# Second layer's edge-relation rows: one bf16 product over 48 rows in place of an f32 product over 16

## The chip, the cores and the metric

One core of one Trainium2 chip runs the whole program. The metric is the device time of one execution in microseconds; the time of the kernel before is a median of three runs. A profile is one further execution, taken by the hardware profiler.

## What is computed

Four graph layers on 6,250 nodes of 128 features, with 206,250 edges sorted by destination. After each of the first three layers `x = layernorm(x + layer(x))`; the last adds its layer likewise.

- Layer 0 is attention over the edges of each node (GAT), layer 3 a filter made from 50 edge attributes (SchNet).
- Layer 1 (GCN) gathers the row of each edge's source and sums by destination: `out = segment_sum(dinv[src]*dinv[dst]*h[src], dst)`.
- Layer 2 (HGT) is attention with eight heads, in which every edge has one of 16 relation types:

```python
attn = einsum('ehd,ehd->eh', Q[edge_dst], K[edge_src])
attn = attn * rel_scale[edge_rel] / sqrt(DH)      # rel_scale is 16 x 8, DH is 16
```

The change concerns `rel_scale[edge_rel] / sqrt(DH)`, eight numbers for each edge. They depend on no node, and the kernel makes them ahead of layer 2, while layer 1's edges are summed.

## The kernel before

Edges are taken in 1,616 tiles of 128, in 101 rounds of 16 tiles (`ROUND`). A round has four slots (`SLOTS`) of four tiles (`KT`). All five engines run programs of their own, tied by semaphores; each layer's edge stage is a block of such programs between barriers. Every program is in the kernel twice, for narrow and wide windows of destinations (`either`); in the profiled execution it was the narrow one, a straight list of 101 rounds.

The edge stage of layer 1 (lines 1102 to 1270), per round:

- GpSimd issues 16 indirect DMAs (line 1153), one for each tile, each fetching 128 rows of `gcn_table` by `src_idx`. The target is a ring of eight slots, two rounds deep; before it refills a slot it waits on `agg`, which TensorE raises when the sums of that slot are done.
- SyncE loads the round's 2,048 relation types, broadcast to 16 partitions (`load_types`, line 1131), into one of two buffers: partitions 0 to 15 or 32 to 47 of `types`. A buffer is refilled after VectorE has read it (`ty_done`). Ahead of the stage's loop SyncE also loads the weights of layer 2 (lines 1136 to 1139).
- VectorE compares the types with the partition's number (`edge_types`, line 1215), giving a one-hot `oh16` in f32, 16 rows by 2,048, again at partitions 0 or 32; compares destinations for the one-hot `oh` of 128 by 2,048 (`edge_onehot`, line 1210); and adds the round's sums from PSUM to the accumulator `AC` (line 1228).
- TensorE first makes the relation rows: 16 products, one for each tile, of `oh16` (16 rows by 128 edges) with the table `rel_rows` (16 rows by 8), line 1169, then raises `rel_mm`. Then come the round's sums: 16 products of gathered rows with one-hots, 128 by 128, line 1181, each slot after its gathers (`gath`). Both are f32, and an f32 product stands in the trace as two pairs of weight load (PEld) and matmul (PE); 16 products are 32 of each. TensorE waits besides for `ty_done`, `rel_kept` (a PSUM buffer copied out), `oh_done` and `acc_step` (a PSUM bank added).
- ScalarE copies the relation rows out of PSUM (line 1199) and stores them to `relation_rows` every four rounds.

The table comes in at the start of the program (line 265), is scaled by 1/4 there by VectorE (line 391), and is copied once more to partitions 32 to 47 at the head of the edge stage (line 1264). At that head VectorE also clears buffers and makes the rows of node types (`type_rows`, lines 1238 to 1253), all before the first `edge_types`.

Of the kernel before, what the change touches and what calls it, by code (L numbers as in the profile page):

```python
# [16 lines left out]
BF16 = mybir.dt.bfloat16  # L17
I32 = mybir.dt.int32
U32 = mybir.dt.uint32
ALU = mybir.AluOpType  # L20
# [3 lines left out]
P = 128  # L24
# [5 lines left out]
NR = -(-E // (P * ROUND))  # L30
# [8 lines left out]
NC = -(-(N + P) // CN)  # L39
# [15 lines left out]
NTYPE, NREL, NG = 8, 16, 50  # L55
TY = 64 + NTYPE
# [52 lines left out]
def build(nc, a, out):  # L109
    ctx = ExitStack()  # L110
    with ctx:
# [24 lines left out]
        def sems(name, n=SLOTS):  # L136
            return [sem(f"{name}{b}") for b in range(n)]
# [56 lines left out]
        rel_rows = rows[:, 2 * P:2 * P + H2]  # L194
        rel = rel_rows[0:NREL, :]
# [21 lines left out]
        ld_x, ld_rel = sems("start_x", NC), sem("start_rel")  # L217
# [37 lines left out]
        with nc.Block() as block:  # L255
            @block.sync
            def _(sp):
# [7 lines left out]
                sp.dma_start(rel, a["L2_gnn_rel_scale"]).then_inc(ld_rel, 16)  # L265
# [71 lines left out]
            def _(dve):  # L337
# [52 lines left out]
                dve.wait_ge(ld_rel, 16)  # L390
                s.mark(dve.tensor_scalar(rel, rel, 1.0 / float(np.sqrt(C2)), None, ALU.mult))
# [624 lines left out]
        with nc.Block() as block:  # L1016
# [56 lines left out]
            def _(dve):  # L1073
# [16 lines left out]
                with dve.Fori(0, NC) as c:  # L1090
# [3 lines left out]
                    for j in range(PARTS):  # L1094
# [8 lines left out]
        ty_ready, ty_done, rel_mm, rel_kept, rel_stored = (sems("gcn_edge_types", 2), sem("gcn_type_onehot"), sem("gcn_rel_product"), sem("gcn_rel_kept"),  # L1103
                                                           sems("gcn_rel_stored", 2))
        A = Arena(TMP, 0, TW)
# [3 lines left out]
        types = A.take(RW, parts=2 * 32, dtype=I32)  # L1109
        oh16 = A.take(RW, parts=2 * 32)  # L1110
# [10 lines left out]
        iota_ps, rel_iota = PS[3][:, 1, 0:P], PS[3][:, 1, P:P + 1]  # L1121
        rel_ps = [PS[2][:, j, 0:ROUND * H2].rearrange("p (t h) -> p t h", h=H2) for j in range(2)]

        def kind_rows(par):
            return slice(32 * par, 32 * par + NREL)

        with nc.Block() as block:
            @block.sync
            def _(sp):
                def load_types(i):  # L1130
                    sp.dma_start(types[kind_rows(i % 2), :], a["rel_row"][0, i * RW:(i + 1) * RW].partition_broadcast(NREL)).then_inc(ty_ready[i % 2], 16)

                for i in range(2):
                    load_types(i)
# [8 lines left out]
                for i in range(NR - 2):  # L1143
                    sp.wait_ge(ty_done, i + 1)
                    load_types(i + 2)
# [11 lines left out]
            def _(pe):  # L1157
# [5 lines left out]
                def program(narrow):  # L1163
                    def round_(j, i, par, last):
# [3 lines left out]
                        for t in range(ROUND):  # L1168
                            m = nc.tensor.matmul(rel_ps[par][:, t, :], oh16[kind_rows(par), t * P:(t + 1) * P], rel_rows[kind_rows(par), :], start=True, stop=True)  # L1169
# [38 lines left out]
            def _(dve):  # L1208
# [4 lines left out]
                def edge_types(j, i, par):  # L1213
                    dve.wait_ge(ty_ready[par], 16 * (j + 1))
                    dve.tensor_tensor(oh16[kind_rows(par), :], types[kind_rows(par), :], rel_iota[kind_rows(par), :].to_broadcast([NREL, RW]), ALU.is_equal).then_inc(ty_done, 1)

                def program(narrow):
                    def round_(j, i, par, last):
                        if not last:
                            dve.wait_ge(rel_mm, i + 1)  # L1220
                            edge_types(j + par, i + 1, 1 - par)
                            dve.wait_ge(agg, (i + 1) * SLOTS)
                            edge_onehot(i + 1, 1 - par)
# [10 lines left out]
                    edge_types(0, 0, 0)  # L1234
                    edge_onehot(0, 0)
                    rounds(dve, round_, narrow)

# [1074 lines left out]
```

## Time and profile before

| | us |
|---|---|
| median of 3 runs | 11,816.71 (11,815.05 to 11,828.76) |
| profiled execution, time | 11,788.6 |
| profiled execution, span from first to last instruction | 11,786.7 |
| TensorE matmuls busy | 6,487.3 (55%) |
| GpSimd busy | 6,158.0 (52%) |
| TensorE weight loads busy | 5,541.6 (47%) |
| VectorE busy | 4,881.6 (41%) |
| ScalarE busy | 1,784.6 (15%) |

No engine is busy throughout, since four edge stages with different limits follow each other. In order of time the gathers of the four run from 52 to 3,112, 3,486 to 5,810, 5,966 to 8,713 and 9,194 to 11,632 us; the second is the one that is changed. Busy shares of the whole span say little about it, and it has to be read by itself. Matmul ends in the trace are modelled, so the time at which TensorE had really finished is better read from the engine that waited for it.

### The profile page before, as it was taken

Reading aid. Unit: us, or ns where it says so; the run is one execution under the profiler, and the core shown is the slowest. Engines: PE = TensorE matmul, PEld = TensorE weight load, DVE = VectorE, ACT = ScalarE, POOL = GpSimd, SP = SyncE. Lnnn points to the kernel's source line nnn. Section 1 sums busy time; section 2 is a strip of 40 time slices with the busy share of each in tenths; the row PEclk is TensorE's granted clock in tenths of the full one; section 3 lists DMA queues with packets and bytes.
Section 4 is the critical chain, followed back from the end, with each engine's and each line's share of the span. In section 5 each row is a group of like instructions: output and inputs, shape, how many; then the busy total and the mean of one; then the engine's idle time right before and its main releaser. Section 6 shows DMA issues by size and latency. Waiting matters only on the chain. (4 is left out here: it accounts for less than half of the span.)

```text
span 11786.7 us, 95611 instructions
## 1 busy us (share of the span) xinstructions
PE 6487.3 (55%) x31067; PEld 5541.6 (47%) x31067; DVE 4881.6 (41%) x10538; ACT 1784.6 (15%) x2785; POOL 6158.0 (52%) x6479
## 2 busy tenths in 40 slices
PE   4555555555435555555544445444443677777775
PEld 4444444444425555555434444444432455555553
DVE  4444444444552222222345555555555344444444
ACT  0000000000110000000110000000011444444443
POOL 4544544554216666666445555555530566666663
PEclk6666666666555555555566666666655677777776
DMA  4222222222111111111133433333320222222221
GB/s 132 72 75 74 73 75 75 72 75 75 42 26 55 54 55 55 54 55 54 44 123 121 124 121 119 121 120 122 120 69 1 65 62 61 61 60 61 62 61 38
DMA packets 388329, 878.63 MB, mean 75 GB/s; under 512 B 134341, under 2 KB 202872, under 8 KB 368224
## 3 DMA queue, kind: packets, MB, share of 16 engines
q0 software_dynamic: 232704, 536.56, 16.5%
q1 hardware_dynamic: 150242, 324.95, 8.3%
q10 hardware_dynamic: 4896, 11.01, 0.2%
q8 instruction: 258, 4.23, 0.1%
q14 instruction: 229, 1.88, 0.1%
HBM read 839.65 MB, written 32.40 MB: 74 GB/s over the span
## 5 line engine op out<-in xcount | busy, mean ns | idle before, releaser
L621 POOL DMA_INDIRECT PM<-gat_table,src_idx x1616 | 1529.1, 946 | 1579.9 <-PE ps L660 1070.4
L2081 POOL DMA_INDIRECT TMP<-schnet_table,src_idx x1616 | 1563.3, 967 | 1355.5 <-DVEq L2183 481.8
L1595 POOL DMA_INDIRECT PM<-hgt_kv_table,src_idx x1616 | 1531.4, 948 | 1371.3 <-PE ps L1627 752.0
L1153 POOL DMA_INDIRECT PM<-gcn_table,src_idx x1004 | 953.0, 949 | 463.8 <-issue 288.6
L1169 PE MATMUL ps<-rows,xT 16*128 16x8 f32 x3232 | 625.6, 301 | 716.3 <-issue 696.0
L1169 PEld LDWEIGHTS ps<-rows,xT 16*128 16x128 f32 x3232 | 646.2, 277 | 702.8 <-issue 671.7
L1153 POOL DMA_INDIRECT TMP<-gcn_table,src_idx x612 | 578.6, 945 | 702.4 <-POOLq L1016 373.9
L2108 PE MATMUL ps<-PM 128*128 128x128 f32 x3232 | 627.8, 357 | 539.6 <-issue 402.7
L2108 PEld LDWEIGHTS ps<-PM 128*128 128x128 f32 x3232 | 571.7, 266 | 582.3 <-issue 581.9
L1627 PE MATMUL ps<-PM 128*128 128x136 f32 x3232 | 608.8, 353 | 337.5 <-DVE PM L1716 322.1
L1228 DVE TENSOR_TENSOR AC<-AC,ps 128x128 f32 x101 | 29.2, 289 | 1829.8 <-remote 1437.0
L639 PE MATMUL ps<-PM 128*128 128x4 f32 x3232 | 697.6, 339 | 101.9 <-issue 71.9
L1627 PEld LDWEIGHTS ps<-PM 128*128 128x128 f32 x3232 | 557.8, 253 | 374.6 <-DVE PM L1702 345.1
L639 PEld LDWEIGHTS ps<-PM 128*128 128x128 f32 x3232 | 662.3, 304 | 134.1 <-issue 90.1
L1610 PE MATMUL ps<-TMP 128*128 128x128 f32 x3232 | 654.2, 367 | 59.0 <-issue 24.4
L660 PE MATMUL ps<-PM 128*128 128x137 f32 x3232 | 644.2, 377 | 0.3 <-issue 0.3
L1610 PEld LDWEIGHTS ps<-TMP 128*128 128x128 f32 x3232 | 585.5, 271 | 91.0 <-issue 37.8
L2153 DVE TENSOR_TENSOR PM<-ps,TMP 128x512 f32<-128x512 f32 x404 | 277.2, 686 | 830.9 <-remote 609.4
L660 PEld LDWEIGHTS ps<-PM 128*128 128x128 f32 x3232 | 618.7, 281 | 3.0 <-issue 0.3
L2091 PE MATMUL ps<-PM,WA 50*128 50x512 f32 x808 | 595.3, 825 | 11.1 <-DMA PM<-in_attrT 11.1
L689 PE MATMUL ps<-ident,TMP 64*128 64x64 f32 x101 | 36.8, 365 | 1011.3 <-DVE TMP L813 844.4
L2098 PEld LDWEIGHTS ps<-WA,PM 128*128 128x128 f32 x3232 | 566.2, 246 | 35.8 <-issue 14.8
(374 smaller groups left out, 10772.4 us busy)
## 6 DMA issues: line engine op xcount, KB each, us to landing
PM<-local_dst_row SPq DMA_DIRECT2D x101, 1024.0 KB
PM<-local_dst_row SPq DMA_DIRECT2D x202, 512.0 KB
PM<-in_attrT SPq DMA_DIRECT2D x101, 400.0 KB
PM<-gat_table,src_idx POOLq DMA_INDIRECT x1616
PM<-hgt_kv_table,src_idx POOLq DMA_INDIRECT x1616
TMP<-schnet_table,src_idx POOLq DMA_INDIRECT x1616
PM<-gcn_table,src_idx POOLq DMA_INDIRECT x1004
xT<-in_rel_row SPq DMA_DIRECT2D x101, 128.0 KB
```

The lines of the kernel that those rows point to most:

```text
L621: pool.indirect_dma_start(out=g[:, par, t, 0:ROW0], out_offset=None, in_=tab0_d, in_offset=bass.IndirectOffsetOnAxis(ap=src_idx[:, i * ROU ...
L639: m = nc.tensor.matmul(adp[:, t * H0:(t + 1) * H0], ohT[:, b % 2, k * P:(k + 1) * P], window_of(narrow, adw, i, b, k), start=True, stop=True)
L660: m = nc.tensor.matmul(PS[1][:, bank, 0:GW], o, row_, start=start, stop=stop)
L1153: pool.indirect_dma_start(out=g[n % DEEP][:, k, :], out_offset=None, in_=tab1_d, in_offset=bass.IndirectOffsetOnAxis(ap=src_idx[:, n * KT ...
L1169: m = nc.tensor.matmul(rel_ps[par][:, t, :], oh16[kind_rows(par), t * P:(t + 1) * P], rel_rows[kind_rows(par), :], start=True, stop=True)
L1595: pool.indirect_dma_start(out=g[:, par, t, 0:2 * P], out_offset=None, in_=kv_d, in_offset=bass.IndirectOffsetOnAxis(ap=src_idx[:, i * ROUN ...
L1610: m = nc.tensor.matmul(q_ps[b % 2][:, k, :], ohT[:, b % 2, k * P:(k + 1) * P], window_of(narrow, qw, i, b, k), start=True, stop=True)
L1627: m = nc.tensor.matmul(sums_ps, o, row_, start=b % 2 == 0 and k == 0, stop=b % 2 == 1 and k == KT - 1)
L2081: pool.indirect_dma_start(out=g[:, b, k, :], out_offset=None, in_=tab3_d, in_offset=bass.IndirectOffsetOnAxis(ap=src_idx[:, (i * SLOTS + b ...
L2091: nc.tensor.matmul(zb[b], w1, attr[:, par, b * KT * P:(b + 1) * KT * P], start=True, stop=True).then_inc(z_mm, 1)
L2098: m = nc.tensor.matmul(wb[b % 2][:, k, :], soft[:, b % 2, k * P:(k + 1) * P], w2, start=False, stop=(k == KT - 1), skip_group_check=True)
L2108: m = nc.tensor.matmul(sb_[bank][:, c:c + P], msg[:, b % 2, k, :], oh[:, b % 2, k, :], start=start, stop=stop)
```

## The change

1. The table. It is no longer loaded and scaled at the start of the program. At the head of the edge stage SyncE loads it three times, to rows 0 to 15, 16 to 31 and 32 to 47 of `rel`. `rel_pieces` scales it and splits it in place: `relb` is its value in bf16; what that leaves over is taken on in rows 16 to 47, and what is left over once more in rows 32 to 47. The three groups of rows then hold three bf16 pieces whose sum is the f32 value exactly.
2. The product. One bf16 product over 48 rows in place of the f32 product over 16 rows: 16 products a round as before.
3. The one-hot of types is 48 rows by 2,048 in bf16 (each of the three groups the same), in two buffers by free position. VectorE's compare has the same length and reads types as int32 as before.
4. The types are broadcast to 48 partitions in place of 16, into a single buffer in place of two; a load is issued when VectorE has read the one before it.

```diff
-        types = A.take(RW, parts=2 * 32, dtype=I32)
-        oh16 = A.take(RW, parts=2 * 32)
+        types = A.take(RW, parts=KINDS, dtype=I32)
+        oh16 = A.take(2, RW, parts=KINDS, dtype=BF16)
+        rel, relf, relb = A.take(H2, parts=KINDS), A.take(H2, parts=KINDS), A.take(H2, parts=KINDS, dtype=BF16)
...
-                    sp.dma_start(types[kind_rows(i % 2), :], a["rel_row"][0, i * RW:(i + 1) * RW].partition_broadcast(NREL)).then_inc(ty_ready[i % 2], 16)
-
-                for i in range(2):
-                    load_types(i)
+                    sp.dma_start(types, a["rel_row"][0, i * RW:(i + 1) * RW].partition_broadcast(KINDS)).then_inc(ty_ready, 16)
+
+                for j in range(PIECES):
+                    sp.dma_start(rel[j * NREL:(j + 1) * NREL, :], a["L2_gnn_rel_scale"]).then_inc(rel_ld, 16)
+                load_types(0)
...
-                for i in range(NR - 2):
+                for i in range(NR - 1):
                     sp.wait_ge(ty_done, i + 1)
-                    load_types(i + 2)
+                    load_types(i + 1)
...
-                            m = nc.tensor.matmul(rel_ps[par][:, t, :], oh16[kind_rows(par), t * P:(t + 1) * P], rel_rows[kind_rows(par), :], start=True, stop=True)
+                            m = nc.tensor.matmul(rel_ps[par][:, t, :], oh16[:, par, t * P:(t + 1) * P], relb, start=True, stop=True)
...
-                    dve.wait_ge(ty_ready[par], 16 * (j + 1))
-                    dve.tensor_tensor(oh16[kind_rows(par), :], types[kind_rows(par), :], rel_iota[kind_rows(par), :].to_broadcast([NREL, RW]), ALU.is_equal).then_inc(ty_done, 1)
+                    dve.wait_ge(ty_ready, 16 * (i + 1))
+                    dve.tensor_tensor(oh16[:, par, :], types, rel_iota.to_broadcast([KINDS, RW]), ALU.is_equal).then_inc(ty_done, 1)
...
+                def rel_pieces():
+                    s = Steps(dve, rel_done)
+                    for j in range(2):
+                        s.link(dve.tensor_scalar(above[:, j:j + 1], iota_p[0:KINDS, :], float((j + 1) * NREL), -1.0, ALU.is_ge, ALU.mult))
+                    s.link(dve.scalar_tensor_tensor(kind, above[:, 0:1], float(NREL), iota_p[0:KINDS, :], ALU.mult, ALU.add))
+                    s.mark(dve.scalar_tensor_tensor(rel_iota, above[:, 1:2], float(NREL), kind, ALU.mult, ALU.add))
+                    dve.wait_ge(rel_ld, 16 * PIECES)
+                    s.link(dve.tensor_scalar(rel, rel, 1.0 / float(np.sqrt(C2)), None, ALU.mult))
+                    for j in range(PIECES - 1):
+                        s.link(dve.tensor_copy(relb, rel))
+                        s.link(dve.tensor_copy(relf, relb))
+                        s.link(dve.scalar_tensor_tensor(rel, relf, above[:, j:j + 1], rel, ALU.mult, ALU.add))
+                    s.link(dve.tensor_copy(relb, rel))
...
-                for par in range(2):
-                    dve.tensor_copy(rel_iota[kind_rows(par), :], iota_p[0:NREL, :]).then_inc(acc_step, 1)
-                dve.tensor_copy(rel_rows[kind_rows(1), :], rel).then_inc(acc_step, 1)
-                dve.wait_ge(acc_step, 5)
-                dve.sem_inc(acc_step, 3)
+                dve.wait_ge(acc_step, 2)
+                dve.sem_inc(acc_step, 6)
+                rel_pieces()
                 dve.sem_inc(rel_mm, 1)
                 type_rows()
```

## Rows read from the trace of the kernel before

**Rows 1.** Two stretches: us; busy (count) of PE, PEld, DVE, ACT, POOL; PEclk, DMA, GB/s.
```profile
52.00:3112.00 3060.00, 1584.52 (x8173) 1466.27 (x8173) 1268.12 (x3785) 145.22 (x695) 1528.47 (x1616) 0.61 0.25 75
3486.00:5811.00 2325.00, 1320.77 (x6409) 1276.04 (x6409) 500.39 (x322) 26.62 (x100) 1531.69 (x1616) 0.59 0.19 55
```

**Rows 2.** Waits, 3520 to 5830 us: who waited <- for what: total us, times, longest.
```profile
PE ps L1169 <- issue: 696.0, 676, 2.6
...
POOL PM L1153 <- issue: 284.9, 934, 0.4
PE ps L1181 <- issue: 279.2, 355, 2.4
...
POOL TMP L1153 <- issue: 167.6, 549, 0.4
POOL PM L1153 <- remote: 148.1, 51, 4.0
POOL TMP L1153 <- remote: 132.5, 42, 4.0
POOL PM L1153 <- PE ps L1181: 27.2, 7, 5.0
POOL TMP L1153 <- PE ps L1181: 25.0, 9, 4.9
```

**Rows 3.** Timeline near 4,510 us: start us, us, instruction, count [idle before <-releaser].
```profile
4499.88 0.95 POOL L1153 DMA_INDIRECT TMP<-gcn_table,src_idx  x1 [3.79 <-PE ps L1181]
...
4503.65 4.96 PE L1169 MATMUL ps<-rows,xT 16*128 16x8 f32 x32
...
4518.32 0.27 ACT L1199 COPY xT<-ps 128x128 f32<-128x128 f32 x1 [19.01 <-remote]
...
4518.64 0.94 POOL L1153 DMA_INDIRECT PM<-gcn_table,src_idx  x1 [0.30 <-issue]
...
4522.83 0.94 POOL L1153 DMA_INDIRECT PM<-gcn_table,src_idx  x1 [3.25 <-remote]
```

**Rows 4.** TensorE under known granted clock, three short stretches (columns as in rows 1).
```profile
3512.60:3519.50 6.90, 6.86 (x32) 6.86 (x32) 6.76 (x3) 0.00 (x0) 5.38 (x6) 0.50 0.37 97
4503.70:4505.90 2.20, 2.20 (x21) 2.20 (x21) 2.04 (x2) 0.00 (x0) 1.83 (x2) 1.00 0.21 60
4528.80:4533.00 4.20, 4.20 (x20) 4.18 (x20) 0.00 (x0) 0.04 (x1) 3.00 (x4) 0.50 0.16 47
```

**Rows 5.** Lines of the whole span: a product in bf16, L2096 in the last layer.
```profile
L2096 PE MATMUL ps<-typ 96*128 96x512 bf16 x404 | 191.3, 473 | 63.0 <-DVE PM L2147 54.3 <-issue 8.2
...
L2096 PEld LDWEIGHTS ps<-typ 96*128 96x128 bf16 x404 | 40.0, 99 | 478.9 <-issue 357.6 <-DVE PM L2147 121.3
```

**Rows 6.** Timeline at the head of layer 1's edge stage.
```profile
3486.27 0.94 POOL L1153 DMA_INDIRECT TMP<-gcn_table,src_idx  x1 [373.94 <-POOLq L1016]
...
3499.85 0.16 DVE L1264 COPY rows<-rows 16x8 f32<-16x8 f32 x1
...
3501.56 0.35 DVE L1248 CAST WA<-xT 8x384 bf16<-8x384 f32 x1
...
3505.68 3.97 POOL L1153 DMA_INDIRECT PM<-gcn_table,src_idx  x1 [0.30 <-issue]
3505.98 3.55 DVE L1253 TENSOR_SCALAR PM<-PM,cols 72x6400 bf16<-72x6400 int32 x1 [1.04 <-DMA PM<-in_type_row]
...
3512.64 6.99 PE L1169 MATMUL ps<-rows,xT 16*128 16x8 f32 x32 [17.78 <-DVE xT L1215]
```

**Rows 7.** Timeline at the end of that stage: last gather, last add.
```profile
5809.28 0.94 POOL L1153 DMA_INDIRECT PM<-gcn_table,src_idx  x1 [0.30 <-issue]
...
5824.65 0.29 DVE L1228 TENSOR_TENSOR AC<-AC,ps 128x128 f32 x1 [10.84 <-PE ps L1181]
```

**Rows 8.** Line 1215 by itself: durations ns min/median/max, first and last start.
```profile
L1215 DVE TENSOR_TENSOR xT<-xT,ps x101: 2267/2274/2281, 3510.3 to 5794.1; 16x2048 f32<-16x2048 int32 x101
```

**Rows 9.** Line 265 by itself: the present load of the table, issue to landing.
```profile
DMA to landing us min/median/max: 21.7/21.7/21.7
```

More of the change, by code:

```diff
@@ L55 @@
 NTYPE, NREL, NG = 8, 16, 50
+PIECES = 3
 TY = 64 + NTYPE
@@ L192, in psv @@
                 f"p ({' '.join(names)}) -> p {' '.join(names)}", **dict(zip(names, dims)))
-        rel_rows = rows[:, 2 * P:2 * P + H2]
-        rel = rel_rows[0:NREL, :]
         ref_b = cols[:, 8:12].rearrange("p (a b) -> p a b", a=2)
@@ L216, in build @@
             sem("start_first"), sem("start_round_first"), sem("start_new"), sem("start_late"), sem("start_src"))
-        ld_x, ld_rel = sems("start_x", NC), sem("start_rel")
+        ld_x = sems("start_x", NC)
         c0, v0, w_ready, rows_ready, brk_done, mm, evac, st0 = (sem("start_consts"), sem("start_dve"), sem("start_w_ready"), sem("start_rows_ready"),
@@ L1102, in build @@
         gath, oh_done, agg, acc_step = sems("gcn_gathered", DEEP), sem("gcn_onehot"), sem("gcn_sums"), sem("gcn_added")
-        ty_ready, ty_done, rel_mm, rel_kept, rel_stored = (sems("gcn_edge_types", 2), sem("gcn_type_onehot"), sem("gcn_rel_product"), sem("gcn_rel_kept"),
+        ty_ready, ty_done, rel_mm, rel_kept, rel_stored = (sem("gcn_edge_types"), sem("gcn_type_onehot"), sem("gcn_rel_product"), sem("gcn_rel_kept"),
                                                            sems("gcn_rel_stored", 2))
+        rel_ld, rel_done = sem("gcn_rel_loads"), sem("gcn_rel_pieces")
         A = Arena(TMP, 0, TW)
@@ L1108, in build @@
         A = Arena(xT, 0, NP)
-        types = A.take(RW, parts=2 * 32, dtype=I32)
-        oh16 = A.take(RW, parts=2 * 32)
+        KINDS = PIECES * NREL
+        types = A.take(RW, parts=KINDS, dtype=I32)
+        oh16 = A.take(2, RW, parts=KINDS, dtype=BF16)
+        rel, relf, relb = A.take(H2, parts=KINDS), A.take(H2, parts=KINDS), A.take(H2, parts=KINDS, dtype=BF16)
+        above, kind = A.take(2, parts=KINDS), A.take(1, parts=KINDS)
         relw = A.take(2, 4, ROUND, H2)
@@ L1120, in build @@
         type_of = cols[0:TY, NTYPE:NTYPE + 1]
-        iota_ps, rel_iota = PS[3][:, 1, 0:P], PS[3][:, 1, P:P + 1]
+        iota_ps, rel_iota = PS[3][:, 1, 0:P], PS[3][0:KINDS, 1, P:P + 1]
         rel_ps = [PS[2][:, j, 0:ROUND * H2].rearrange("p (t h) -> p t h", h=H2) for j in range(2)]
-        def kind_rows(par):
-            return slice(32 * par, 32 * par + NREL)
         with nc.Block() as block:
@@ L1211, in edge_onehot, with edge_types @@
                                       over(lr[:, bass.ds(i * ROUND, ROUND)], P, ROUND, P), ALU.is_equal).then_inc(oh_done, 1)
[L1213 to L1215 removed]
+                def edge_types(i, par):
+                    dve.wait_ge(ty_ready, 16 * (i + 1))
+                    dve.tensor_tensor(oh16[:, par, :], types, rel_iota.to_broadcast([KINDS, RW]), ALU.is_equal).then_inc(ty_done, 1)
                 def program(narrow):
@@ L1220, in round_ @@
                             dve.wait_ge(rel_mm, i + 1)
-                            edge_types(j + par, i + 1, 1 - par)
+                            edge_types(i + 1, 1 - par)
                             dve.wait_ge(agg, (i + 1) * SLOTS)
@@ L1232, in round_ @@
                                            lambda bank, c: PS[bank][:, 0, c:c + P])
-                    edge_types(0, 0, 0)
+                    edge_types(0, 0)
                     edge_onehot(0, 0)
                     rounds(dve, round_, narrow)
+                def rel_pieces():
[11 more added lines that the diff above has]
+                    s.link(dve.tensor_copy(relb, rel))
                 def type_rows():
```

3 lines of the change are left out of this document (removed).

## The prediction

> **What bounds the kernel now.** I read the page's slices first: the four edge stages follow one another, so the change can only act in layer 1's, and the rest of the program is taken as it is. Next came the busy times of that stretch beside layer 0's [rows 1]. Both hold 1,616 gathers with 1,530 us of GpSimd work, but layer 1's takes 2,325 us, 23.0 us for each of its 101 rounds. No engine is busy all of it.
>
> The list of waits tells who waits for whom [rows 2]. GpSimd's idle time has two kinds. 1,483 times it sat idle for 452.5 us (284.9 + 167.6) with nothing to wait for: 0.305 us each, its own gap between two gathers. With 0.946 us for a gather (1,531.69 / 1,616 is 0.948) [rows 1] a gather costs 1.25 us however fast the others are, and a round 16 x 1.25 = 20.0 us. The other kind is 109 waits, about one a round, of 332.8 us together (148.1 + 132.5 + 27.2 + 25.0), put down to TensorE or to "remote". Line 1153 waits for one thing only, `agg`: a slot of the ring summed by TensorE. So GpSimd has run its two rounds ahead and waits for TensorE, 3.05 us a time (two of them stand in [rows 3]).
>
> TensorE in turn waits for no other engine: its idle time reads "issue", 696.0 us ahead of line 1169 and 279.2 us ahead of line 1181 [rows 2]. It is the engine that sets the end of this stage, by little: 23.0 us a round against GpSimd's 20.0.
>
> Why it needs 23.0 us is only half seen. Fed without a break, 32 f32 pairs of line 1169 take 6.9 us at a granted clock of 0.50, the 1.2 GHz level, so 0.216 us each; 20 pairs, all of line 1181, take 4.2 us at the same level, 0.21 each; at the 2.4 GHz level it is 21 in 2.2 us, 0.105 each [rows 4]. The stage's mean clock is 0.59 [rows 1], so a round of 64 pairs costs 13.6 us at most. The "issue" gaps are 975.2 / 101 = 9.7 us a round on top, and 13.6 + 9.7 = 23.3 is about the 23.0 seen. The trace gives no releaser for these gaps. Nor are the recorded ends to be trusted: the 32 products recorded as done at 4,508.6 us let ScalarE go at 4,518.32 [rows 3]. Somewhere TensorE's stream of f32 pairs stalls; I treat the gaps as a cost of that stream and keep their fate open.
>
> **Part 1, the product (the gain).** Per round 32 f32 pairs of line 1169 go, 16 bf16 pairs come. The new pair's price is not in the trace. Bounds: below, 0.10 us, the bf16 weight load of line 2096 [rows 5]; above, 0.47 us, the matmul of the same line, which streams 512 columns where ours streams 8 [rows 5]. It is nearest to the short f32 pair with the same 8 columns, 0.216 us [rows 4], and I take that: 3.5 us a round (1.6 to 7.6). With the sums' 32 x 0.21 = 6.7 us TensorE's own work is 10.2 us. If all 9.7 us of gaps stayed, it would come to 19.9 us, just under GpSimd's 20.0; if they follow the number of pairs (48 for 64), to 10.2 + 7.3 = 17.5. Either way GpSimd becomes the bound and its 109 waits go. Each still leaves the normal gap of 0.305, so the gain is 332.8 - 109 x 0.305 = 299.6 us. More can't come from a cheaper product: GpSimd's 20.0 us a round are late next.
>
> **Part 2, the end of the stage.** Now TensorE trails by up to two rounds: the last gather starts at 5,809.3, ends at 5,810.2, and the last add starts at 5,824.65 [rows 7], 14.4 us later. With TensorE caught up only the last slot's landing and 8 pairs (1.7 us) are left. The landing is not in the rows; I put the whole tail at 6 us (between 2 and 14.4), a gain of 8.
>
> **Part 3, the head of the stage.** Three copies go (0.16 us each, [rows 6]), twelve linked steps of at most 8 columns come, between 0.16 and 0.35 us each [rows 6], so 1.4 to 3.7 us, say 2, before VectorE's types of round 0 and with them TensorE's first product, now at 3,512.64 [rows 6]. What covers it: GpSimd's first gather starts at 3,486.27 [rows 6] and it may issue 32 before it needs a slot back, so until 3,486.3 + 40 + 3 = 3,529 (the 3 is below). TensorE's first slot is done by 3,512.6 + 2 + 3.5 + 1.7 = 3,520. Cost 0, with 9 us of cover; if that cover were gone, 2 us once. SyncE has three loads of the table ahead and one load of types fewer, two issues more, ahead of the weights of layer 2; these aren't used until `type_rows`. The load and scaling that leave the start of the program are one DMA and one step of about 0.15 us on engines whose work there ends in other loads: 0.
>
> **Part 4, the types.** VectorE's compare goes from 16 to 48 partitions at the same 2,048 columns. Line 1215 takes 2.274 us for 16 partitions [rows 8], and its twin on 128 partitions is as long: in the 6.9 us of the first stretch VectorE is busy 6.76 with three instructions [rows 4]. Cost 0; VectorE has 500 us of work in the 2,325 [rows 1]. The single buffer puts a load's landing between two compares: behind the waiting compare stand that round's one-hot and the previous add, and TensorE waits for both. A load has a round less 2.3 us for the compare, 17.7 us, to land. The load of 128 KB itself grows to 384 KB; the stage moves 55 GB/s with the DMA engines 0.19 busy, layer 0's 75 GB/s at 0.25 [rows 1], so 256 KB more in 20 us (13 GB/s) finds room. Cost 0, and below 0 there is nothing to gain.
>
> **Sum.** 11,788.6 (profiled execution) - 299.6 - 8 + 0 = 11,481. The median of the runs lies 28.1 us above the profiled time; if that stays, 11,509 us, 2.6% less. That is the forecast.
>
> **Rivals.**
> - *Part of the waits stays.* The gaps in TensorE come in bursts, and where one outlasts the ring's two rounds GpSimd waits as now (longest wait 5.0 us, [rows 2]). For it: their cause is unknown. Against it: 10.2 us of work leave it half of each round to catch up. With half of the 299.6 us left, 11,659.
> - *VectorE holds GpSimd back.* At the head of the stage [rows 6] one gather takes 3.97 us instead of 0.95 while line 1253, a one-input step with bf16 out, runs for 3.55 us: 0.85 of that step is lost to GpSimd. If the new compare, now with bf16 out as well, did the same, each round would lose 0.85 x 2.27 = 1.93 us, 195 us in all, and the time be 11,704. Against it: the compare has two inputs, one of them in PSUM, and with f32 out it leaves gathers at 0.95 [rows 3]. The Trainium skill bears on this in two places. "SBUF — State Buffer", section "Who interferes with whom", calls the port pair that VectorE shares with GpSimd an exclusive lock; the gather of 3.97 us agrees. "VectorE: DVE Perf Modes", section "Why `tensor_tensor` can't do 2×_2P or 4×", says a two-input step never takes both ports for one tensor, by which this rival is out and the sum stays; no row here shows such a step with bf16 out.
> - *No change.* The gaps are set by something outside TensorE's instructions and grow to fill the round, or the bf16 pair costs as much as two f32 ones. The second needs 0.43 us a pair, near the upper bound, and a round would still be 13.6 + 9.7. Time 11,817, give or take 24. The recorded gaps, 42% of the stage without a releaser, are what speaks for it.
> - *Slower.* The single buffer makes a ring: compare (2.3), issue (0.3), landing, compare. It decides once a landing takes over 20.4 us, as round and ring are then 23.0. The one landing of a small load that the trace gives is 21.7 us [rows 9]; that one stood behind megabytes of other loads, which this stage hasn't. With it a round is 24.3 us, 101 x 1.3 = 131 us more: 11,948.
>
> **How the numbers follow.** Forecast 0.67, part of the waits 0.13, VectorE holding GpSimd 0.05, no change 0.09, slower 0.06. The forecast's own spread is 11,475 (median no longer 28 us above the profile) to 11,560. To leave out 2 in 10 the range takes in the second case to its upper half: 11,470 to 11,690. A measurement of this kernel can tell about 0.2% (24 us) from no change: faster 0.85, same 0.09, slower 0.06.
>
> **What would show it.** In the profile after: gathers of line 1153 at 1.25 us apart with almost no waits between, the stage from first to last gather in 1,615 x 1.25 + 3 = 2,022 us; line 1169 with 1,616 bf16 pairs; TensorE idle ahead of line 1181 with a gather's DMA as releaser; compare still 2.27 us; last add within 6 us of the last gather. If instead the waits on `agg` remain, part 1 is wrong; if gathers grow longer beside line 1215's successor, part 4.

## The result, and the profile after

The changed kernel takes 11,799.3 us (median of 17 runs) against 11,823.6 for the kernel before (17 runs): a ratio of 0.998, interval 0.9973 to 0.9988. That is 24 us, where the forecast was 308 and its range ended at 11,690.

The numbers below can't be read without one thing. These programs were met in two kinds of execution. In some sessions the kernel before took 9,286 to 9,304 us, in others 11,674 to 11,682, and 11,824 in the main comparison. Two of the chips (numbers 14 and 15) showed both kinds in different sessions, so it goes neither with the kernel nor with the chip's number. I call them the 9.3 ms kind and the 11.7 ms kind. Both profiles of the main comparison are of the second, and the forecast was made from one.

Layer 0's edge stage after, then layer 1's, as in [rows 1]:

```profile
52.00:3148.00 3096.00, 1584.98 (x8173) 1466.77 (x8173) 1267.22 (x3785) 145.01 (x695) 1524.34 (x1616) 0.61 0.27 74
3522.00:5824.00 2302.00, 872.13 (x4826) 717.57 (x4826) 493.85 (x331) 26.53 (x100) 1527.50 (x1616) 0.57 0.29 67
```

From its first to its last gather layer 1's stage takes 2,300.7 us (3,521.76 to 5,822.44); before it took 2,323.0 ([rows 6], [rows 7]), 22.3 more. The profiled execution itself is no shorter (span 11,810.8), mainly because layer 0's stage, where nothing changed, was 36 us longer in it. TensorE has 449 us less work (872 for 1,321), and the stage didn't follow. Its waits, as in [rows 2]:

```profile
PE ps L1179 <- issue: 1185.4, 854, 3.9
...
POOL PM L1151 <- issue: 295.1, 954, 1.8
PE ps L1167 <- issue: 204.3, 224, 2.6
POOL TMP L1151 <- issue: 179.6, 589, 0.4
POOL PM L1151 <- remote: 176.9, 41, 6.0
POOL TMP L1151 <- remote: 63.5, 15, 6.1
...
POOL PM L1151 <- PE ps L1179: 32.6, 9, 6.0
POOL TMP L1151 <- PE ps L1179: 26.1, 7, 6.0
```

The sums are now line 1179 (1181 before), the product 1167 (1169), the gather 1151 (1153). Two things are to be seen. TensorE's "issue" gaps were 975.2 us and are 1,389.7 (1,185.4 + 204.3): 13.8 us a round where they were 9.7. They took up nearly all that the change freed. And GpSimd still waits for TensorE: 72 waits of 299.1 us in all, for 109 of 332.8. The waits are fewer and longer. The prediction named waits on `agg` that remain as the sign that part 1 is wrong. The timeline shows what stands in the gap before one; the second number in a row is the duration, the brackets give the idle time before:

```profile
4571.26 0.94 POOL L1151 DMA_INDIRECT TMP<-gcn_table,src_idx  x1 [6.00 <-remote]
...
4602.44 0.37 PE L1179 MATMUL ps<-TMP 128*128 128x128 f32 x1 [2.43 <-issue]
4603.84 0.29 PEld L1179 LDWEIGHTS ps<-TMP 128*128 128x128 f32 x1 [2.51 <-issue]
4604.97 0.94 POOL L1151 DMA_INDIRECT PM<-gcn_table,src_idx  x1 [0.30 <-issue]
4605.24 0.37 PE L1179 MATMUL ps<-TMP 128*128 128x128 f32 x1 [2.43 <-issue]
...
4610.39 0.94 POOL L1151 DMA_INDIRECT PM<-gcn_table,src_idx  x1 [4.47 <-remote]
...
4610.84 1.24 PE L1179 MATMUL ps<-TMP 128*128 128x128 f32 x5 [0.33 <-issue]
```

Towards the end of 28 gathers in a row (4,571.3 to 4,605.9) TensorE starts a weight load or a matmul every 1.40 us, each of 0.29 or 0.37 us. GpSimd has used up its ring at 4,605.9 and stops, and within 5 us TensorE runs without gaps again. I call the first a slow stretch. Starts within it are nearly all 0.70 us or a multiple of it apart.

### The profile page after: what moved, and what is told of

Same layout as the page of the kernel before. It is cut to its first block and busy times, and to the rows that moved or that the text cites. A ratio compares the mean times of both kernels' runs of the same rounds, so it can differ in the third digit from the quotient of the medians.

```text
span 11810.8 us, 92389 instructions
## 1 busy us (share of the span) xinstructions
PE 6015.8 (51%) x29451; PEld 4961.5 (42%) x29451; DVE 4873.4 (41%) x10546; ACT 1783.8 (15%) x2785; POOL 6141.8 (52%) x6479
## 3 DMA queue, kind: packets, MB, share of 16 engines
q0 software_dynamic: 232704, 536.56, 17.9%
## 5 line engine op out<-in xcount | busy, mean ns | idle before, releaser
L1179 PE MATMUL ps<-TMP,PM 128*128 128x128 f32 x2008 | 503.8, 374 | 755.3 <-issue 747.8
L1179 PEld LDWEIGHTS ps<-TMP,PM 128*128 128x128 f32 x2008 | 416.5, 274 | 833.7 <-issue 832.5
```

Of the source, the lines that this page charges most:

```text
L1179: m = nc.tensor.matmul(PS[par][:, 0, 0:P], row_, o, start=b + k == 0, stop=b + k == SLOTS + KT - 2)
```

## The experiments

Where a run leaves part of the work out, its expectation says which part. A stage is the time from the first to the last of layer 1's gathers.

**In the 9.3 ms kind.** The first four runs were meant to find TensorE's lateness by taking away parts of it. The edits, in this order (the lines that adapt waits and operands are left out): two of a slot's four gathers; one of its four sum products; a ring half as deep; a loop in TensorE's program.

```
-                    for k in range(KT):                   # gathers of a slot
+                    for k in range(KT // 2):
...
-                            for k in range(KT):           # products of a slot
+                            for k in range(1):
...
-                    if n >= DEEP:
-                        pool.wait_ge(agg, n - DEEP + 1 + SLOTS)
+                    if n >= DEEP // 2:
+                        pool.wait_ge(agg, n - DEEP // 2 + 1 + SLOTS)
...
-                    rounds(pe, round_, narrow)
+                    by_pairs(pe, round_)
```

> The changed kernel with two of a slot's four gathers left out; each gathered tile is multiplied twice, so TensorE has as many products as before and GpSimd half its gathers (the second layer's sums are not the reference's). Three theories are set against each other. HELD BACK: TensorE stalls while gathers run back to back, and is let go when the full ring stops them. STREAM: the stalls belong to TensorE's own stream of instructions. GATHERS ALONE: in a timed execution GpSimd's 1.25 us a gather sets the stage in both kernels, and TensorE's stalls are seen under the profiler only. HELD BACK and GATHERS ALONE: 8 x 1.25 = 10.0 us of gathers a round cover TensorE's 8.5 (6.7 for the sums, 1.8 for the bf16 rows), the stage from first to last gather falls from 2,301 us to 1,010 to 1,100, the program to 10,500 to 10,600. STREAM: TensorE's 8.5 us and its 13.8 us of gaps a round stay, 22.3 us a round, the program at 11,750 or above.

> The changed kernel with all gathers, but only one of a slot's four sum products (the second layer's sums are not the reference's): TensorE has 4 f32 products a round in place of 16, besides the 16 in bf16. HELD BACK: what holds TensorE is in the gathers, not in its work; the stalls stay and the program stays within 60 us of the changed kernel's 11,799. GATHERS ALONE: no change either, within 25 us. STREAM: 50 instructions a round in place of 98 halve the gaps of 13.8 us, TensorE needs 1.7 + 1.8 + 7 = 10.5 us a round, GpSimd's 20.0 us become the bound, the program falls by 260 to 280 us to about 11,530.

> The changed kernel whole, but GpSimd waits before a gather until the slot four (not eight) before it is summed: the ring is one round deep. HELD BACK: every 16 gathers (20 us) the ring is full and a stall of 4 to 6 us follows, where it now follows 32 gathers: 24 to 26 us a round, the program 100 to 300 us slower, 11,900 to 12,100. GATHERS ALONE: TensorE needs 8.5 of 20 us and keeps up with one round of lead: no change within 25 us of 11,799. STREAM: 22.3 us a round as now with less slack, 0 to 150 us slower.

> The changed kernel whole, but TensorE's 101 rounds of this stage are a loop over pairs of rounds in place of a straight list, so its instructions are fetched once. STREAM (if fetching is what stalls it): the gaps of 13.8 us a round go, GpSimd's 20.0 us a round bound the stage, 2,022 us from first to last gather, the program 11,520 to 11,550. HELD BACK and GATHERS ALONE: no change within 25 us of 11,799, and under HELD BACK the profile shows the same stalls.

Stages: 1,020, 2,020, 2,028 and 2,020 us; ratios to the kernel before 0.892 (0.8908 to 0.8937), 1.000 (0.9991 to 1.001), 1.0011 (1.0001 to 1.002), 1.0002 (0.9992 to 1.0011). The numbers expected were all for the 11.7 ms kind, so these runs decide nothing between HELD BACK and STREAM there. Nothing but fewer gathers moves the time by more than 9 us: 1,615 x 1.25 = 2,019 us is GpSimd's own time, and TensorE is hardly ever late (GpSimd waits for it 14 us in the run with the short ring, 39 us in the one with half of the gathers, at most 1 us in the others). The waits of the loop version, of the same kind in the other two with all gathers:

```profile
PE ps L1179 <- DMA PM<-gcn_table,src_idx: 697.3, 247, 5.0
...
POOL PM L1151 <- issue: 304.4, 999, 0.3
...
POOL TMP L1151 <- issue: 182.8, 600, 0.3
```

That is the picture that the forecast had for the changed kernel. The question was now what the change is worth there.

> The changed kernel as it is. In the four runs before this one, on another chip than the first comparison's, the kernel before took 9,289 us in place of 11,824, and all four edge stages ran at GpSimd's pace. Two theories. CHIP STALL: on the first chip something stalls TensorE's instructions in both kernels; where it is absent GpSimd's 16 x 1.25 = 20.0 us a round bound the second layer's stage with the f32 product (13.7 us of TensorE work) as with the bf16 one (about 7.5), so the change is worth 0 within 0.1% there: 9,285 to 9,295 beside 9,289. HIDDEN GAIN: the kernel before still waits there for TensorE and the change takes that away: more than 20 us less. If this run falls on a chip with the stalls, both kernels are again near 11,800 and the ratio is near 0.998.

> The kernel BEFORE with two of a slot's four gathers left out, each gathered tile multiplied twice (the second layer's sums are not the reference's). GpSimd needs 10.0 us a round, so TensorE's f32 work is laid open. CHIP STALL, on a chip without stalls: 32 + 32 f32 pairs at 0.213 us are 13.6 us a round at the 1.2 GHz level and 7.1 at 2.4; the stage takes 10 to 13.8 us a round, so the program 0 to 380 us more than the changed kernel with the same half of gathers (8,287), most likely 8,600. HIDDEN GAIN makes the same difference and more. On a chip with stalls: 19 to 23 us a round, as the stalls set the pace whatever GpSimd does.

> The changed kernel with the same two of four gathers left out (as e1_half_gathers), beside e6_before_half on the same chip. On a chip without stalls 8,287 us again. On a chip with stalls this tells whether back-to-back gathers bring them on: if they do, the stage falls to about 10 us a round (program 10,500 to 10,600); if the stalls are TensorE's whatever GpSimd does, it stays near 22 us a round (11,750).

> The kernel BEFORE with three of a slot's four gathers left out, the gathered tile multiplied four times (the second layer's sums are not the reference's): GpSimd needs 5.0 us a round, so TensorE's work bounds the stage. On a chip without stalls: 64 f32 pairs at 0.111 us (2.4 GHz level, as the stage ran mostly with half of the gathers) are 7.1 us a round, 720 us for the stage, at most 1,380 at the 1.2 GHz level; the program about 7,990 to 8,100, that is 300 to 190 less than with half the gathers (8,290). On a chip with stalls, if back-to-back gathers bring them on: the gathers are rarely back to back, about the same 7 to 14 us a round; if they are TensorE's own: about 20.

> The CHANGED kernel with the same three of four gathers left out. This prices the change where TensorE is the bound: 32 f32 pairs at 0.111 us (or 0.213) and 16 bf16 pairs at 0.028 us (as recorded in e4_pe_loop) are 4.0 us (7.3 at the lower clock) a round, below GpSimd's 5.0 and VectorE's 4.9, so 5.1 to 7.3 us a round: the program 200 us less than e8_before_quarter, at least 120. On a chip with stalls the difference is smaller if they grow into the time freed, as they did in the first comparison (9.7 to 13.8 us a round).

The unedited changed kernel: 9,287.89 us against 9,286.62, ratio 1.0001 (0.9992 to 1.001), as CHIP STALL had it. With half of the gathers: 8,290.3 before, 8,287.6 after, stages 1,025 and 1,019; the 8,600 that was called most likely was wrong, since TensorE ran at a mean granted clock of 0.75 and not near 0.50. With a quarter, 5 us of GpSimd a round, TensorE becomes the bound and the change shows: 8,265.4 and 8,027.2 us, stages 979.7 and 737.5. The stretches (columns as in [rows 1]), the first of before with a quarter, the second of after:

```profile
2460.00:3440.00 980.00, 974.56 (x6464) 960.02 (x6464) 482.21 (x304) 26.77 (x101) 373.29 (x396) 0.76 0.17 48
```

```profile
2460.00:3200.00 740.00, 533.36 (x4856) 507.95 (x4856) 479.28 (x312) 26.87 (x101) 374.40 (x396) 0.85 0.47 99
```

So before's whole stream of 64 f32 pairs needs 9.7 us a round when nothing keeps it waiting, at a granted clock of 0.76, not the 23.3 that the prediction gave it; and it has almost no gaps (974.56 of 980 busy). The run's own expectation, 7,990 to 8,100 us for the program, had counted on the 2.4 GHz level and was missed. After, TensorE isn't the bound; a row of the waits names what is:

```profile
DVE xT L1213 <- DMA xT<-in_rel_row: 248.2, 100, 3.5
```

The compare waits 2.5 us a round for its single buffer to be loaded: the ring of the fourth rival, at 7.3 us a round and far from the 23 from which it would have decided.

Two more runs made TensorE late by ordinary work, to see whether the change then pays as the sum had it: 44 spare f32 products in each round.

```
+                        for _ in range(44):
+                            nc.tensor.matmul(PS[0][:, 1, 0:P], ident[:, :], ones[:, :], start=True, stop=True)
```

> The kernel BEFORE, whole, with 44 further f32 products of constants a round in TensorE's program, into a PSUM bank nobody reads. It makes TensorE the bound of the stage by about what the first comparison's profile shows (23.0 us a round against GpSimd's 20.0), this time by ordinary work. TensorE has 64 + 88 pairs; at the 0.152 us of e8_before_quarter (9.7 us for 64) that is 23.1 us a round, the stage 2,340 us against 2,022, the program 9,590 to 9,640 on a chip without stalls. If TensorE stays at the 2.4 GHz level (0.111 us) it is 16.9 us and nothing changes.

> The CHANGED kernel with the same 44 products a round. ORDINARY WORK (the prediction's reading: TensorE's lateness is a sum of work and gaps from which the change takes its share): 120 f32 pairs at 0.152 us and 16 bf16 at 0.028 are 18.7 us a round, GpSimd's 20.0 bound the stage again, and the program is at 9,290 to 9,310, some 300 us below e10_before_padded. So the mechanism works where TensorE is late with work. If it saves only 20 us here too, as in the first comparison, the fault is in that mechanism and not in the nature of the gaps.

Before with them 9,339.6 us (1.0057, 1.0038 to 1.0077), after with them 9,288.8 (1.0003, 0.9993 to 1.0013). The lateness came out at 0.4 us a round instead of 3, and the forecasts of 9,590 to 9,640 and of some 300 us saved were missed. Under a mean granted clock of 0.84 a pair took 0.134 us (2,033 us for 15,167), not the 0.152 that was counted on:

```profile
2460.00:4500.00 2040.00, 2033.23 (x15167) 2018.88 (x15168) 484.55 (x302) 26.50 (x100) 1509.88 (x1598) 0.84 0.23 62
```

2,033 of 2,040 us busy, and GpSimd waits. What there was of it, 51 us, the change took away whole. So the step of the sum holds, at this small size, where TensorE is late by work.

**In the 11.7 ms kind.** Run 12 met it again. It is the third run's kernel, the ring one round deep. Runs 12 to 15 are one execution each, and the kernel before beside them one, so their totals have no interval; what they show is in their traces.

> The changed kernel with a ring one round deep again (16 gathers in flight in place of 32), as one look. The edge stages tell which kind of chip it is. Where the kernel before takes about 9,290 us: 2,020 to 2,030 us for layer 1's stage, as in the first such run, and nothing new. Where it takes about 11,800 us, TensorE falling behind while gathers run, until the ring is full and GpSimd stops: theory A, a TensorE that is held back by gathers in flight, has GpSimd stop sooner, waits of 2 to 3 us in place of 4.1 and more of them, and a stage of 2,200 to 2,350 us; theory B, a TensorE that is late by a lag of its own of some 10 to 15 us whatever is in flight, has the stage at 2,500 us or more, since 16 gathers (20 us) cover less of the lag than 32 do (40 us).

11,655.7 us against 11,679.7, the stage 2,294.0. One cycle of its TensorE, of 45.5 us, and the start of the next, in six windows (columns as in [rows 1]):

```profile
4575.00:4590.00 15.00, 6.93 (x42) 6.05 (x41) 4.68 (x3) 0.53 (x2) 11.07 (x12) 0.50 0.35 75
4590.00:4607.00 17.00, 6.95 (x41) 6.08 (x42) 0.00 (x0) 0.00 (x0) 12.73 (x15) 0.50 0.20 51
4608.00:4615.00 7.00, 1.15 (x4) 0.68 (x3) 3.35 (x3) 0.00 (x0) 4.50 (x5) 0.50 0.18 47
4615.00:4620.00 5.00, 1.17 (x4) 0.93 (x4) 1.32 (x1) 0.00 (x0) 1.16 (x2) 0.50 0.53 105
4621.00:4636.00 15.00, 6.99 (x44) 6.12 (x42) 4.68 (x3) 0.27 (x1) 11.32 (x12) 0.50 0.37 92
4636.00:4653.00 17.00, 7.32 (x43) 6.45 (x44) 0.00 (x0) 0.00 (x0) 13.00 (x14) 0.50 0.21 55
```

For 32 us TensorE keeps up (some 42 pairs in 15 us, then it waits for gathers), for the next 12 it does 8 pairs, GpSimd stops, and it begins anew. The granted clock is 0.50 throughout, so this isn't the clock. With the shorter ring the slow stretch lasts 12 us in place of 31 and 37 in two cycles of the changed kernel, and ends at GpSimd's stop in both; the period and the stop (5.5 us) are nearly the same. Theory A had the end of the slow stretch and the stage right, and the size of the waits wrong (it had 2 to 3 us, and more of them); theory B is out. Three runs asked what decides the stop.

```
+                    if n % SLOTS == 0:                    # e13: ahead of each round's gathers
+                        for j in range(2):
+                            if n or j:
+                                pool.wait_ge(paused, 2 * (n // SLOTS) + j)
+                            pool.memset(PM[:, 12200:12900], 0.0).then_inc(paused, 1)
```

> The changed kernel with a pause in GpSimd's gathers: before each round's 16 gathers two small fills of an unused stretch (700 columns each), about 1.5 to 2 us a round, 150 to 200 us in all. On a chip where the kernel before takes about 9,290 us nothing covers it: layer 1's stage goes from 2,020 to some 2,190. Where it takes about 11,700 (the kind of chip of the two main profiles), TensorE's instructions come one per 0.7 us after GpSimd has issued gathers for a while, until the ring makes GpSimd stop. Theory A, a break in the gathers is what lets TensorE's stream recover: the short break in each round takes the place of the waits on `agg`, and the stage is 2,150 to 2,300 us, not longer than the 2,294 without it, with GpSimd's waits well under 285 us. Theory B, the break is of no use, and TensorE's slow stretches come by something else: the waits stay and the pauses come on top, 2,400 us and more.

> The changed kernel with TensorE's rounds of this stage as a loop over pairs of rounds in place of a straight program, once more. On a chip at about 9,290 us: 2,020 us as before. On one at about 11,700: if TensorE's slow stretches come from fetching its instructions (each new one from memory, with the gathers in the way), a loop changes them: they go (stage 2,020 to 2,100) or, if each jump back costs a fetch, they change their place to the start of each pair of rounds, and the number of waits follows the 50 jumps. If they have nothing to do with the fetch of instructions: 2,300 us and the same picture as in the straight program.

> The changed kernel with one of each slot's four sum products, three quarters of the sums left out (24 fewer TensorE instructions' pairs in each round: 20 in place of 32 + 16 = 48 - 24 = 24). On a chip at about 9,290 us: 2,020 us as before. On one at about 11,700: if TensorE gets a limited number of instructions while gathers run, some 2 a us and about 110 more at each stop of GpSimd, the 40 or 48 instructions of a round in place of 96 need no stop at all, and the stage is 2,020 to 2,060 us. If it is held up for 12 us or more every two rounds whatever it has to do: 2,250 us or more.

(A round of the last has 16 bf16 pairs and 8 f32 pairs, 48 weight loads and matmuls.) The kernel before took 11,673.7 beside all three; they took 11,691.6, 11,661.0 and 11,630.8, with stages of 2,323.0, 2,286.6 and 2,270.7 us. A stage less GpSimd's own 2,018.8 (1,615 x 1.25) is what its stops cost: 304 in the kernel before, 282 after, 275 with the short ring, 268 with the loop, 252 with a quarter of the sums. The first two are from the main comparison, where layer 0's stage, the same in all, took 3,060 and 3,096 us for 3,003 to 3,007 in the runs since; so differences of some ten us among these five say little.

The loop hardly alters the stops in number and length: GpSimd stops 49 times so long that two gathers start over 4 us apart, in the changed kernel 53 times. It does fix their place. 48 of them come ahead of the same gather of a pair of rounds, in the changed kernel 23, and that was the sign that its expectation gave for a fetch at each jump back. But the run with a quarter of the sums has its stops as regularly without a loop (25 of 25 ahead of a round's first gather, 64 gathers apart), and the packets that carry instructions say the rest. Instruction queues of the changed kernel from 3,540 to 5,700 us (packets, MB, share), then all that the loop version has there:

```profile
q8 instruction: 37, 0.61, 0.1%
q14 instruction: 21, 0.17, 0.0%
```

```profile
q14 instruction: 20, 0.16, 0.0%
```

With the loop, the one edit, queue 8 carries nothing, and TensorE is held up as before. So it isn't the fetching of its instructions from memory.

With a quarter of the sums, half of TensorE's instructions, the stops' sum falls by about a tenth; but they come once in four rounds, each nearly twice as long. The waits of e15 and, from its timeline, TensorE on the cheapest instructions of the stage:

```profile
POOL TMP L1151 <- PE ps L1179: 255.3, 25, 10.4
```

```profile
4503.82 0.10 PEld L1167 LDWEIGHTS ps<-xT 48*128 48x128 bf16 x1 [2.70 <-issue]
4505.22 0.16 PE L1167 MATMUL ps<-xT 48*128 48x8 bf16 x1 [2.64 <-issue]
4506.62 0.10 PEld L1167 LDWEIGHTS ps<-xT 48*128 48x128 bf16 x1 [2.70 <-issue]
...
4511.86 0.94 POOL L1151 DMA_INDIRECT TMP<-gcn_table,src_idx  x1 [10.39 <-PE ps L1179]
```

A 0.10 us weight load takes its 1.40 us as an f32 one does. My model of a limited number of instructions per us, which gave 2,020 to 2,060, is out. The pauses were 1.44 us of fills (1.3 more between two gathers), 131 us in all. The stage grew by 22 us over the changed kernel's 2,300.7 (29 over run 12's), not by 131: 304 - 131 = 173 us of waits are left of 282. It is 23 above theory A's range and 77 below theory B's. 131 us of pauses took the place of 109 us of stops, so a break in the gathers, whoever makes it, counts for most of its length. A break of 1.3 us doesn't end the stops, though: they come every three rounds in place of two, and still last 5.3 us. So the gathers were varied next, by the first edit of all.

> The changed kernel with half of the gathers left out (two of each slot's four; the sums read each row twice), for the kind of execution in which the whole program takes about 11,700 us. There the waits of GpSimd in all variants of layer 1's stage so far come once per 20, 40 or 80 us of gathers and last 3.0, 5.5 and 10.1 us. Theory A, the loss is a share of the time in which gathers are issued (0.6 us + 0.12 of it): GpSimd issues 10 us a round, loses 1.2 to 1.8, and the stage is 1,130 to 1,190 us. Theory B, the loss is one of each round's work on TensorE whatever the gathers take (2.5 to 3 us a round): 1,260 to 1,320 us or more. If the execution is of the other kind (9,290 us for the kernel before): 1,010 us as before.

> The kernel before with half of the gathers left out, for the same kind of execution. With its TensorE at 23.3 us a round, as the prediction had it, and unchanged by the gathers left out, the stage is 2,300 us and the change is worth 1,100 of them. Theory A (TensorE is slow only while gathers run, and only so long that GpSimd loses about an eighth): 1,150 to 1,250 us, and little between the two kernels. Theory B: 1,300 to 1,400.

> The changed kernel with one of each slot's four gathers (three quarters left out), for the same kind of execution. On the other kind it takes 737 us, where VectorE and the load of types are the bound. Theory A: 5 us of gathers a round lose 0.6 to 1.2, which VectorE's round hides: 740 to 800 us. Theory B: 2.5 to 3 us more in each round: 950 us and more.

10,539.6, 10,551.0 and 10,108.0 us, beside 11,682.3 for the kernel before (ratios 0.902, 0.903 and 0.865, each within 0.003); stages 1,174.1, 1,189.7 and 735.4 us. The first two fall into theory A's ranges, the third 5 us below its own; none is near theory B's. Waits of the kernel before with half of the gathers, the last two those of TensorE, and one of GpSimd's stops:

```profile
POOL TMP L1153 <- PE ps L1181: 84.7, 45, 2.7
...
POOL PM L1153 <- PE ps L1181: 81.8, 43, 2.5
...
PE ps L1181 <- issue: 51.2, 85, 1.6
...
PE ps L1169 <- issue: 40.7, 79, 1.2
```

```profile
3995.06 0.95 POOL L1153 DMA_INDIRECT PM<-gcn_table,src_idx  x1 [0.30 <-issue]
3997.99 0.95 POOL L1153 DMA_INDIRECT TMP<-gcn_table,src_idx  x1 [1.98 <-PE ps L1181]
```

TensorE's gaps without a releaser, 9.7 us a round in the whole kernel [rows 2], are under 1 us a round here (91.9 us in some 96 rounds). The stop is 1.7 us longer than the normal gap and comes each 11.7 us. Side by side (a stop is what it has over the normal gap; for the kernel before it is the mean of a round, 304 / 101):

| | gathers between two stops, us | a stop, us |
|---|---|---|
| before, half of the gathers | 10 | 1.7 |
| before | 20 | 3.0 |
| after | 40 | 5.7 |
| after, a quarter of the sums | 80 | 10.1 |

That is 0.5 us and 0.12 of the gathers' time, within 0.4 us; nearly this line (0.6 and 0.12) was on record, from the last three rows, before the runs with half of the gathers. The changed kernel with half of them fits as well: stops of mostly 2.1 to 2.6 us after 15 to 17 us of gathers. In the first row TensorE is 92% busy (1,009.5 of 1,100 us), so its own work has a part in that stop. The table doesn't say what sets the distance between two stops. Counted in TensorE's pairs it is mostly 96 in the changed kernel, with the short ring, with the loop and with a quarter of the sums (2 rounds of 48 or 4 of 24), about 80 in the kernel before and 64 in it with half of the gathers; so fewer pairs make fewer stops, each longer, and about the same sum. And with a quarter of the gathers, where GpSimd issues 5 of the 7.3 us of a round with waits between, the stage is as long as in the 9.3 ms kind (735.4, 737.5): nothing is held up. With half, before's TensorE gets through its 64 f32 pairs in 11.8 us, the same pairs for which the whole kernel needs 23.0.

## Why the prediction was wrong

- *What bounds the kernel: right in its rows, wrong in what they mean.* GpSimd did wait for TensorE, and TensorE for nothing that the trace shows. From that the prediction made 23.3 us a round as what TensorE needs. Before's stream needs 9.7 us when it runs unbroken (e8), and 11.8 or less in the same kind of execution with half of the gathers (e17). TensorE was not slow for its work; it was held up while gathers ran, and under 1 us a round of its gaps is left when half of them go.
- *Part 1 is the step that failed:* "I treat the gaps as a cost of that stream". Its two readings were that the 9.7 us stay or that they follow the number of pairs; they grew to 13.8. The sum took GpSimd's waits as the excess of TensorE's round over 20.0 us, and all 299.6 us of gain hang on that. The runs showed instead that the gaps last until GpSimd stops, and that GpSimd stops only when TensorE is late enough for the ring to be full. Work taken from TensorE makes this later and the stop longer, hardly less in sum: 282 us for 304, not 0. The bf16 pair, taken at 0.216 us (0.10 to 0.47), costs 0.028: 16 of them stand in 0.58 us, the last matmul 0.164 of it. This was below its lower bound, which was a weight load that had not been hidden, and changes nothing: any price would have met the same stops.
- *What the 22 us are.* After, the stop comes mostly once in two rounds, before about once in each. By the fit above one stop fewer in two rounds saves its constant 0.5 us, 25 us in 101 rounds. It agrees with the 22.3, but the fit is made from these stages too; argued, not shown by a run of its own. 22 us is also less than layer 0's stage, which nobody changed, moved between the two profiles (36); what stands is the 24 us of the medians. Half of the gathers give 15.6 (1,189.7 to 1,174.1), also small.
- *Part 2* was right in kind: the last add starts 7.8 us after the last gather's end (5,823.4 to 5,831.18), before 14.4. The tail was put at 6, the gain at 8; it is 6.6.
- *Part 3* held: TensorE's first product comes 27.6 us after the stage's first gather, before 26.4, and no gather waits for it.
- *Part 4* held: the compare is 2.27 us on 48 partitions, and the gathers beside it stay at 0.94:

```profile
L1213 DVE TENSOR_TENSOR xT<-xT,ps x101: 2270/2272/2280, 3547.1 to 5804.7; 48x2048 bf16<-48x2048 int32 x101
```

  The second rival is out by this; the bf16 output, which no row of before showed, changes nothing. The Trainium skill has it so ("VectorE: DVE Perf Modes", section "Why `tensor_tensor` can't do 2×_2P or 4×": a two-input step doesn't take both ports for one tensor), and the 0.94 us agree. The load of types is waited for in 2 of 101 rounds (3.7 us).
- *The rivals.* "No change" had the mechanism in one clause, "set by something outside TensorE's instructions and grow to fill the round", and 0.09. What stood for it was in the rows: 975 us without a releaser are 9.7 of the 23.3 us a round on which the forecast rested, and products recorded as done at 4,508.6 let ScalarE go 10 us later [rows 3]. Another row spoke for it and wasn't read so: layer 0's stage, with the same 1,616 gathers, loses a third of its time beside the same engines [rows 1]. In the 9.3 ms kind that stage takes 2,022 us, so its third was lost in the same way; before the result this could only have raised that chance.
- *The offset.* The median was taken to stay 28.1 us above the profiled time. After the change it lies 13.2 below it, so this term told nothing.
- *The kind of execution.* The forecast has no case for one in which GpSimd alone sets the pace. There the change is worth 0 (0.9992 to 1.001), and 242 us of the stage with a quarter of the gathers.

What stays open: what it is in the chip that holds TensorE up while gathers are issued, and why only in some sessions. Ring depth, fetched instructions and the granted clock (0.50 in slow stretches and between them in run 12) are out as its cause, and its amount of work changes the number of stops but hardly their sum. The runs show that it comes while gathers follow one another without a wait, though not at once (in run 12 TensorE keeps up for 32 us of them), and ends with a break. Longer transfers are out too. The gathers' queue over the whole program, after in the 11.7 ms kind and the same kernel in the 9.3 ms kind (packets, MB, share of 16 DMA engines' span):

```profile
q0 software_dynamic: 232704, 536.56, 17.9%
```

```profile
q0 software_dynamic: 232704, 536.56, 22.7%
```

17.9% of 11,810.8 us and 22.7% of 9,287.8 are 2,114 and 2,108: each engine is busy with them as long in both. What GpSimd does to issue a gather takes as long too (0.94 us in both). Whether the issuing, the transfers or something they share with TensorE's issue holds it up wasn't tried: a run with smaller rows for the same number of gathers would part the first two. Nor does the fit carry over as it stands: layer 0's stage has 20 us of gathers a round and loses 10.

## What to carry to other kernels

Idle time of an engine that has no releaser is not part of what its instructions cost: before an edit is credited with it, find a stretch in which the same stream runs unbroken, or take away the other engine's work and see whether the gaps go with it. Where two engines wait for each other through a ring, ask what each would take if it had nothing beside it: here 20.0 us a round for GpSimd and 9.7 for TensorE, and neither is the 23.0 of the stage, so taking work from TensorE couldn't bring the difference back.

## What the runs showed of the hardware

- The same program takes 9,287 us in one session and 11,680 in another, on chips with the same number. In the second, all four edge stages are stretched (kernel before in the main comparison: 3,060, 2,323, 2,745 and 2,436 us, for 2,019 to 2,032 each in the changed kernel's run 5).
- In that kind, TensorE falls into stretches, while gathers run in an unbroken row, in which its weight loads and matmuls nearly all start 0.70 us or a multiple of it apart, whether they take 0.10 or 0.37 us; it is at full pace again once GpSimd has stopped for some us.
- At the 1.2 GHz level short bf16 pairs (48 x 128 weights, 8 columns) follow one another in 0.028 us, f32 ones of 8 columns in 0.216 [rows 4].
- The granted clock differs with what is left out: 0.50 in the whole changed kernel (882 of 2,021 us busy), 0.76 in the kernel before with a quarter of the gathers (975 of 980), 0.85 in the changed kernel with a quarter (533 of 740), 0.84 in the kernel before with 44 more products (2,033 of 2,040). All are stretches of the 9.3 ms kind, and the busy share doesn't order them. These 44 products in each round, on top of 64 pairs, made the stage 2% longer. The first of the four stretches (columns as in [rows 1]):

```profile
2441.00:4462.00 2021.00, 881.61 (x4842) 763.68 (x4842) 492.50 (x332) 26.78 (x101) 1526.06 (x1615) 0.50 0.33 76
```
